# Mixer stage: order of the work at the change of a unit (gate behind the output product, last output product behind the scores, exponentials one step ahead, output weights split two and two)

## The chip, the core and the metric

One core of one Trainium2 chip runs the whole program. The metric is the device time of one execution in microseconds (us). PE is TensorE (PEld its weight loads), ACT ScalarE, DVE VectorE, POOL GpSimd, SP SyncE, which issues the DMAs.

## What is computed

A block of two layers on x of 2 x 512 tokens by 512 channels: attention, a linear map, then the mixer (a state-space layer) and experts, with layer norms between. The change is in the mixer alone. Per token (after the projections to gate, x, B, C and dt), with P = 128 tokens a chunk in this kernel (the chunk length is free, the result doesn't depend on it):

```
x, B, C = silu(conv4(project(input)))           # 128 heads of 64 channels in 8 groups; B, C of 128 channels per group
cum     = cumsum(-exp(A_log) * dt) within a chunk
scores  = (C B^T) * exp(cum_i - cum_j), i >= j
y       = scores @ (dt * x) + exp(cum) * C @ state + D * x
state   = exp(cum_last) * state + B^T @ (dt * exp(cum_last - cum) * x)
y       = y * silu(gate);  y = y / rms over the 1024 channels of the group
out    += y @ out_w[group]
```

Float32 products are made of float32r parts: split_product makes high*high, high*low and low*high, three matmuls per 128 channels of depth, so each weight or activation exists as a high and a low part.

## The kernel before, in words

The mixer (function mixer) has 8 groups x 2 halves = 16 **units** of 8 heads (512 channels). A unit has 8 steps, c = 0 to 7, one per chunk of 128 tokens (chunks 0 to 3 are the first sequence, 4 to 7 the second). A group is 16 steps, k = 0 to 15; k = 0 and k = 8 are the first steps of units. Group 0 and group 7 are written out, groups 1 to 6 are a hardware loop (eng.Fori in groups, L1182). Every engine has its own program, in order, and they meet in semaphores alone; the order of the work is written out by hand.

Products of one step on PE, in this order: at c = 0 and 4 **flip_x** of the chunk itself (four transposes of the convolved channels into p_flip, L1242); in the first half the score product C B^T and a transpose of B (p_mix, L1280, L1281, called cb); the **gate** product (12 matmuls of 128x512 into p_gate); **flip_y** of the step before (L1251); the product with the carried state (p_inter, L1295, not at c = 0 and 4); one or two **channel products** (12 matmuls each into one of two banks of p_mix), which prepare x channels of the next unit or sequence, or B and C of the next group (class Plan says which; two at k = 0, 12, 13 and 14, one at the others); the **output product** of the step before (project_out, 12 matmuls into p_out); the state product (p_state, L1311, not at c = 3 and 7); flip_x of the next chunk (not at c = 3 and 7); and **intra**, the scores by x (16 matmuls, p_intra, L1321). Intra ends a step in the tables here. Three PSUM buffers matter: p_flip is single, so flip_x waits until the flip before it is read out (flip_out), and p_gate and p_out are single too. All eight banks are in use.

ACT in a step: the decay exponentials (L1379, eight of 128x128, behind a table load), at c = 0 and 4 empty_x (p_flip to x_tokens, L1350), the Silu of the gate (L1386, behind a table load), empty_y (p_flip to the high part of yT, L1358), the square of y (L1360), at c = 7 gate_high_part (L1335), the first tap of each convolution (L744), its Silu (activate, L752), keep_half (p_out to half_out, first half only), empty_x of the next chunk, and at c = 0 out_high_part (L1342), the high parts of the unit's output weights, which waits for the output product of the step before. The group's exponentials (L1371) stand ahead of k = 0.

DVE in a step: the arguments of the next step's decays (L1442), copies of cb (L1496, L1497), y_low_part (low part of yT, L1452, which frees p_flip), the carried part (L1512, L1516), mean_square, the other taps (L764, three per convolution), out_sum (L1470, L1473, second half only), the state (L1537 to L1544), then **y_sum** (L1550, waits for intra), **y_done** (L1554, by the gate), and at c = 0 out_low_part, four instructions (L1423). At k = 15 the next group's tables (decay_logs, L1430 to L1433) and arguments follow y_low_part. At the head of each loop pass stand two copies (L1480, L1481).

POOL in a step: x_to_state (L1595), x_dt (L1599), x_skip (L1602), the decays by cb (L1607, after the exponentials), inverse_rms (L1582), at c = 7 gate_low_part (four of L1574), the low parts of the next unit's gate weights; it signals gate_split, for which the gate product of c = 0 waits. At c = 0 SP loads the output weights after gate_split too.

Names in rows: wq_t is the decay buffer, cum_all the arguments' input, x_channels and bc_channels the convolved channels.

## Time and profile before

| what | us |
|---|---|
| median of 3 runs (range) | 2282.54 (2276.7 to 2284.81) |
| the profiled execution | 2285.04 |
| its span, first to last instruction | 2283.3 |
| PE busy in it | 2109.0 (92%) |
| DVE, ACT, POOL busy | 1667.0, 1443.2, 1130.3 |
| mean granted clock | 0.963 |
| the mixer: end of the first intra to end of the last | 417.5 to 2191.6 |

A row of the windows view has: the stretch in us from the span's start, its length, then the busy time (and number of instructions) of PE, PEld, DVE, ACT and POOL, the granted clock, the share of the DMA engines and GB/s; a sum row adds the lengths and the busy times of several stretches. A row of the timeline has the start, the time from first start to last end of the instructions merged in it, the engine, line, operation, tiles, their number (x), and in brackets the engine's idle time before it with what ended it.

### The profile page before, as it was taken

The numbers are of one execution on the slowest core, as the hardware profiler recorded it, in microseconds if no ns is written. First come the engines' busy times: TensorE is split into PE (matmuls) and PEld (weight loads), VectorE is DVE, ScalarE is ACT, GpSimd is POOL, SyncE is SP. The second block draws the span as 40 slices with busy tenths as digits, with TensorE's granted clock in tenths as the row PEclk, the third lists the DMA queues.
The fourth block names the chain that finished last, engine by engine and source line by source line (L and its number), as shares of the span: only waits on it lengthen the run. The fifth ranks groups of instructions, "written<-read, shape, count | busy, mean of one in ns | idle before, by whom it ended". The sixth has DMA issues, their size and how long they took to land. (4 is left out here: it accounts for less than half of the span.)

```text
span 2283.3 us, 35195 instructions
## 1 busy us (share of the span) xinstructions
PE 2109.0 (92%) x10968; PEld 1645.1 (72%) x10968; DVE 1667.0 (73%) x2864; ACT 1443.2 (63%) x2823; POOL 1130.3 (50%) x976
## 2 busy tenths in 40 slices
PE   8999886899999999999999999999999999999868
PEld 4666575687777777777777777777777777777645
DVE  4777584677876787678768877877787778777766
ACT  1566524676667666766676677666766776677631
POOL 3545140455545564555465546564645465545531
PEclk9899997899999999999999999999999999999979
DMA  4000001312122212221222122212121222121110
GB/s 157 1 0 0 23 29 41 97 59 81 47 87 79 68 42 87 84 70 40 87 79 70 57 78 70 70 62 74 70 70 62 74 70 75 56 74 57 46 36 37
DMA packets 72231, 140.67 MB, mean 62 GB/s; under 512 B 34450, under 2 KB 35474, under 8 KB 67827
## 3 DMA queue, kind: packets, MB, share of 16 engines
q1 hardware_dynamic: 72050, 138.44, 18.4%
q8 instruction: 92, 1.51, 0.3%
q14 instruction: 89, 0.72, 0.1%
HBM read 134.74 MB, written 3.67 MB: 61 GB/s over the span
## 5 line engine op out<-in xcount | busy, mean ns | idle before, releaser
L92 PE MATMUL p_out<-w_out,yT 128*128 128x512 f32 x1536 | 391.5, 406 | 44.9 <-DVE yT L1452 38.7
L92 PEld LDWEIGHTS p_out<-w_out,yT 128*128 128x128 f32 x1536 | 298.1, 196 | 121.0 <-DVE yT L1452 43.4
L92 PE MATMUL p_mix<-x_high,w_x 128*128 128x512 f32 x1024 | 381.8, 434 | 1.4 <-DVE x_low L1028 1.4
L1607 POOL TENSOR_TENSOR wq_t<-wq_t,cb 128x1024 f32<-128x1024 f32 x128 | 325.2, 2541 | 108.5 <-DVE cb L1497 96.0
L764 DVE SCALAR_TENSOR_TENSOR conv<-p_mix,unit_small,conv 128x511 f32<-128x511 f32 (+2 forms) x384 | 287.3, 748 | 96.7 <-ACT conv L744 87.6
L92 PE MATMUL p_gate<-w_gate,x_high 128*128 128x512 f32 x1024 | 342.1, 416 | 13.7 <-POOL w_gate L1574 13.7
L1379 ACT ACTIVATE wq_t<-wq_t,minus_cum 128x128 f32<-128x128 f32 x1024 | 313.9, 389 | 1.4
L752 ACT ACTIVATE x_channels<-conv 128x512 f32<-128x512 f32 x128 | 80.6, 630 | 266.4 <-DVE conv L764 265.7
L1452 DVE TENSOR_TENSOR yT<-p_flip,yT 128x512 fp32r<-128x512 f32 x128 | 88.4, 691 | 216.0 <-ACT yT L1358 216.0
L1321 PEld LDWEIGHTS p_intra<-x_dt,wq_t 128*128 128x128 f32 x2048 | 241.1, 192 | 2.4
L1321 PE MATMUL p_intra<-x_dt,wq_t 128*128 128x64 f32 x2048 | 242.6, 272 | 0.0
L92 PEld LDWEIGHTS p_mix<-x_high,w_x 128*128 128x128 f32 x1024 | 194.0, 190 | 62.2 <-issue 22.2
L92 PEld LDWEIGHTS p_gate<-w_gate,x_high 128*128 128x128 f32 x1024 | 190.5, 196 | 52.1 <-POOL w_gate L1574 15.8
L1595 POOL TENSOR_TENSOR x_to_state<-x_tokens,group_dt_end 128x512 f32<-128x512 f32 x96 | 102.7, 1070 | 251.7 <-ACT x_tokens L1350 237.0
L1442 DVE TENSOR_TENSOR wq_t<-cum_all,group_logs 128x1024 f32<-128x1024 f32 x128 | 218.1, 1704 | 2.6 <-DMA cum_all<-cum_rows 1.3
L783 POOL TENSOR_TENSOR w_x<-w_raw_tiles,w_x 128x512 fp32r<-128x512 f32 x64 | 87.4, 1366 | 251.2 <-DVE w_x L772 251.2
L92 PE MATMUL p_gate<-w_gate,x_low 128*128 128x512 f32 x512 | 207.8, 406 | 0.0
L92 PE MATMUL p_mix<-x_low,w_x 128*128 128x512 f32 x512 | 201.2, 393 | 0.0
L1599 POOL TENSOR_TENSOR x_dt<-x_tokens,group_dt 128x512 f32<-128x512 f32 x128 | 143.8, 1124 | 99.9 <-PE p_intra L1321 99.6
L1602 POOL TENSOR_TENSOR x_skip<-x_tokens,group_skip 128x512 f32<-128x512 f32 x128 | 183.2, 1431 | 0.5 <-DVE y L1550 0.5
L744 ACT ACTIVATE conv<-p_mix,unit_small 128x512 f32<-128x512 f32 x128 | 99.7, 779 | 114.9 <-PE p_mix L92 112.9
L1386 ACT ACT_TABLE_LOAD x128 | 164.2, 1283 | 4.9 <-DVE y L1554 2.7
(228 smaller groups left out, 4179.4 us busy)
## 6 DMA issues: line engine op xcount, KB each, us to landing
cum_all<-cum_rows SPq DMA_DIRECT2D x128, 512.0 KB, 3.7
w_staged<-in_w_gate SPq DMA_DIRECT2D x16, 1024.0 KB, 5.8
w_raw_tiles<-in_w_x SPq DMA_DIRECT2D x64, 256.0 KB, 3.7
w_staged<-in_w_out SPq DMA_DIRECT2D x16, 1024.0 KB, 4.8
w_raw_tiles<-in_w_bc SPq DMA_DIRECT2D x16, 256.0 KB, 2.9
x<-in_x SPq DMA_DIRECT2D x1, 2048.0 KB, 17.4
out<-z SPq DMA_DIRECT2D x8, 256.0 KB, 2.0
wqkv<-in_wqkv SPq DMA_DIRECT2D x4, 384.0 KB, 6.3
```

The lines of the kernel that those rows point to most:

```text
L92: last = pe.matmul(dst, left[a](k), right[b](k), start=k == 0 and n_ == 0, stop=stop and k == tiles - 1 and n_ == 2)
L744: act.activation(self.conv[:, par], self.p_mix[:, bank], ACT.Identity, bias=w[:, TAPS:TAPS + 1], scale=w[:, TAPS - 1:TAPS]).then_inc(self. ...
L764: m = dve.scalar_tensor_tensor(self.conv[:, par, back:], self.p_mix[:, bank, 0:SEQ - back], w[:, TAPS - 1 - back:TAPS - back], self.conv[: ...
L1321: m = pe.matmul(p_intra[:, h * HEAD_P:(h + 1) * HEAD_P], decay[:, k % 2, h], xdt[:, h], start=True, stop=True)
L1379: m = act.activation(decay[:, k % 2, h], decay[:, k % 2, h], ACT.Exp, bias=neg[:, c, head:head + 1])
L1386: act.activation(sg[:], p_gate[:], ACT.Silu).then_inc(sg_done, 1)
L1442: dve.tensor_tensor(decay[:, k % 2], cumB[:], over(logs[:, 0, c, mine], P), ALU.min).then_inc(arg_done, 1)
L1452: dve.tensor_tensor(yT[:, 1].rearrange("p j t -> p (j t)"), p_flip[:], yT[:, 0].rearrange("p j t -> p (j t)").bitcast(F32), ALU.subtract). ...
L1595: pool.tensor_tensor(xs[:], xtok[:], over(dtend[:, c, mine], HEAD_P), ALU.mult).then_inc(xs_done, 1)
L1599: pool.tensor_tensor(xdt[:], xtok[:], over(dtg[:, c, mine], HEAD_P), ALU.mult).then_inc(xdt_done, 1)
L1602: pool.tensor_tensor(xskip[:], xtok[:], over(dg[:, mine], HEAD_P), ALU.mult).then_inc(xskip_done, 1)
L1607: pool.tensor_tensor(decay[:, k % 2], decay[:, k % 2], cb[:, c].unsqueeze(1).to_broadcast([P, UNIT_HEADS, P]), ALU.mult).then_inc(decay_do ...
```

## The change

On PE, at c = 0 flip_y and the first channel product come ahead of flip_x, and the gate product comes last, behind the other channel product and the output product. At c = 7 the output product moves behind intra. On ACT the exponentials of the next step move to the end of c = 7 (those of the next group too), with the Silu of the last convolution of the unit taken into the next c = 0. On DVE the arguments at c = 0 come after y_low_part, the next group's tables after the carried part, out_sum at c = 7 to the end of the step; the output weights' low parts are made two before the state and two at the end. On POOL x_skip at c = 0 comes after the decays. flip_index (which flip frees p_flip for which) follows the new order: flip_x at c = 0 now waits for y_low_part.

```diff
 # tensor
+                        if c == CPS:
+                            first_flip(g, k, first)
                         if half == 0:
...
                         if c == 0:
-                            pe.wait_ge(gate_split, g * 2 + half + 1)
-                        wait(pe, sg_done, s)
-                        split_product(pe, p_gate[:], ...).then_inc(gate_done, 1)
...
+                            if before:
+                                flip_y(*before)
+                            conv_event(*convs[0])
+                            first_flip(g, k, first)
+                            for i, e in convs[1:]:
+                                conv_event(i, e)
+                            if before:
+                                project_out(*before)
+                            project_gate(g, k, cols)
+                        else:
+                            project_gate(g, k, cols)
+                            flip_y(*before)
...
+                            for i, e in convs:
+                                conv_event(i, e)
+                            if c < CHUNKS - 1:
+                                project_out(*before)
...
                         m.then_inc(intra_done, 1)
+                        if c == CHUNKS - 1:
+                            project_out(*before)
 # scalar
+                group_exps(0)
+                decay_exps(0, 0)
...
+                        if c == 0:
+                            if before:
+                                empty_y(*before)
+                                late = [e for e in PLAN.events(*before, False) if e[0][0] != "cb"]
+                                for e, _, index in late:
+                                    front.activate(act, e, index, PLAN.conv_parity(before[1], e))
+                                square_y(*before)
+                            empty_x(g, k)
+                            for i, e in convs:
+                                first_tap(i, *e)
+                            front.activate(act, convs[0][1][0], ...)
+                            wait(act, out_done, s)
+                            out_high_part(g * 2 + half, half)
+                            if half:
+                                keep_half(*before)
+                            for i, (e, _, index) in convs[1:]:
+                                front.activate(act, e, index, PLAN.conv_parity(k, e))
+                            silu_gate(g, k)
+                            empty_x(g, k + 1)
+                            continue
...
+                        if c == CHUNKS - 1:
+                            if half and not last:
+                                group_exps(g + 1)
+                            if not (last and half):
+                                decay_exps(s + 1, (k + 1) % STEPS)
+                            if not half:
+                                keep_half(*before)
+                            continue
 # vector
-                        if k + 1 < STEPS:
+                        early = c > 0 and k + 1 < STEPS
+                        if early:
                             arguments(s + 1, k + 1)
...
+                        if c == 0:
+                            arguments(s + 1, k + 1)
...
+                        if c == 0:
+                            out_low_part(g * 2 + half, half, (0, 1))
                         if feeds(c):
...
+                        if summed and c == CHUNKS - 1:
+                            out_sum(*before)
                         if c == 0:
-                            out_low_part(g * 2 + half, half)
+                            out_low_part(g * 2 + half, half, (2, 3))
 # gpsimd
-                        wait(pool, y_sum, s)
-                        pool.tensor_tensor(xskip[:], ...).then_inc(xskip_done, 1)
+                        if c:
+                            skip_part(s, mine)
                         pool.wait_ge(exp_done, s + 1)
...
+                        if c == 0:
+                            skip_part(s, mine)
```

## Rows read from the trace of the kernel before

**Rows 1.** The page's busy times: PE's share of the span.

```profile
PE 2109.0 (92%) x10968; PEld 1645.1 (72%) x10968; DVE 1667.0 (73%) x2864; ACT 1443.2 (63%) x2823; POOL 1130.3 (50%) x976
```

**Rows 2.** Windows of group 4: steps k = 0, 1, 2, 8, 9, 10.

```profile
1303.11:1324.95 21.84, 18.44 (x84) 14.87 (x84) 12.90 (x23) 12.64 (x24) 11.42 (x9) 0.84 0.22 75
1324.95:1339.30 14.35, 13.23 (x69) 10.29 (x69) 12.04 (x17) 11.14 (x22) 5.63 (x5) 1.00 0.44 98
1339.30:1352.24 12.94, 12.94 (x69) 10.37 (x69) 9.79 (x13) 9.25 (x19) 5.27 (x4) 1.00 0.31 112
1414.74:1428.69 13.95, 12.71 (x68) 10.21 (x68) 6.73 (x10) 10.99 (x22) 8.13 (x7) 1.00 0.32 115
1428.69:1446.45 17.76, 14.52 (x65) 11.15 (x65) 16.49 (x19) 11.14 (x21) 8.30 (x7) 0.90 0.33 104
1446.45:1459.10 12.65, 12.65 (x66) 10.08 (x65) 10.55 (x15) 8.72 (x18) 6.33 (x5) 1.00 0.19 62
```

**Rows 3.** Windows of k = 0 and 1: groups 1 and 7 alone.

```profile
626.51:661.40 34.89, 30.30 (x150) 24.28 (x151) 25.75 (x40) 23.78 (x45) 16.89 (x13) 0.95 0.30 84
1978.83:2015.09 36.26, 31.51 (x151) 25.12 (x151) 26.01 (x40) 23.80 (x45) 17.06 (x13) 0.91 0.27 95
```

**Rows 4.** The same for groups 2 to 6, their sum.

```profile
sum 179.92, PE 157.18 PEld 125.39 DVE 124.61 ACT 119.24 POOL 85.08; mean PE 31.44 PEld 25.08 DVE 24.92 ACT 23.85 POOL 17.02
```

**Rows 5.** Windows of k = 8, 9, 10 of all eight groups, their sum.

```profile
sum 356.42, PE 321.19 PEld 252.72 DVE 268.76 ACT 246.66 POOL 179.26; mean PE 40.15 PEld 31.59 DVE 33.59 ACT 30.83 POOL 22.41
```

**Rows 6.** Timeline, PE's waits at both unit changes of group 4 (in brackets).

```profile
1305.70 0.65 PE L1242 MATMUL p_flip<-ident,x_channels 128*128 128x128 f32 x4 [2.58 <-issue]
...
1307.71 1.22 PE L92 MATMUL p_gate<-w_gate,x_high 128*128 128x512 f32 x2 [0.82 <-POOL w_gate L1574]
...
1438.82 4.60 PE L92 MATMUL p_out<-w_out,yT 128*128 128x512 f32 x12 [3.25 <-DVE yT L1452]
```

**Rows 7.** Timeline at the loop's turn: POOL and DVE.

```profile
1301.75 5.91 POOL L1574 TENSOR_TENSOR w_gate<-w_staged,w_gate 128x512 fp32r<-128x512 f32 x4
...
1305.57 0.97 DVE L1554 TENSOR_TENSOR y<-y,silu_gate 128x512 f32<-128x512 f32 x1
...
1309.39 0.23 DVE L1480 COPY group_dt<-tables_in 128x128 f32<-128x128 f32 x1 [2.85 <-issue]
```

**Rows 8.** Timeline from k = 7 into k = 8: POOL, DVE, ACT.

```profile
1407.32 2.44 POOL L1607 TENSOR_TENSOR wq_t<-wq_t,cb 128x1024 f32<-128x1024 f32 x1 [1.56 <-DVE cb L1497]
...
1411.70 2.32 DVE L764 SCALAR_TENSOR_TENSOR conv<-p_mix,unit_small,conv 128x511 f32<-128x511 f32 x3 [1.34 <-ACT conv L744]
...
1414.78 0.69 DVE L1550 TENSOR_TENSOR y<-p_intra,x_skip 128x512 f32<-128x512 f32 x1 [0.76 <-PE p_intra L1321]
...
1416.48 2.45 ACT L1379 ACTIVATE wq_t<-wq_t,minus_cum 128x128 f32<-128x128 f32 x8
...
1419.43 1.28 ACT L1386 ACT_TABLE_LOAD   x1
...
1420.73 0.60 ACT L1386 ACTIVATE silu_gate<-p_gate 128x512 f32<-128x512 f32 x1
```

**Rows 9.** Timeline: out_low_part at k = 0 and at k = 8, then arguments, y_low_part.

```profile
1326.55 3.52 DVE L1423 SCALAR_TENSOR_TENSOR w_out<-w_staged,unit_small,w_out 128x512 fp32r<-128x512 f32 x4
...
1430.58 6.45 DVE L1423 SCALAR_TENSOR_TENSOR w_out<-w_staged,unit_small,w_out 128x512 fp32r<-128x512 f32 x4
...
1436.95 1.21 DVE L1442 TENSOR_TENSOR wq_t<-cum_all,group_logs 128x1024 f32<-128x1024 f32 x1
...
1438.09 0.68 DVE L1452 TENSOR_TENSOR yT<-p_flip,yT 128x512 fp32r<-128x512 f32 x1
```

**Rows 10.** Timeline, PE at the mixer's first gate product, first and last output product.

```profile
403.64 1.22 PE L92 MATMUL p_gate<-w_gate,x_high 128*128 128x512 f32 x2 [4.95 <-POOL w_gate L1574]
...
428.25 0.93 PE L92 MATMUL p_out<-w_out,yT 128*128 128x512 f32 x3 [3.47 <-DVE yT L1452]
...
2195.27 5.48 PE L92 MATMUL p_out<-w_out,yT 128*128 128x512 f32 x12 [1.42 <-DVE yT L1452]
```

More of the change, by code:

```diff
@@ L1261, in project_out, with first_flip, project_gate @@
                                   [lambda j, i=i: wo[:, i, j] for i in range(2)], UT).then_inc(out_done, 1)
+                def first_flip(g, k, first):
+                    pe.wait_ge(conv_done, len(PLAN.first) if first and k == 0 else
+                               PLAN.ready(g, k - 1, ("x", UT - 1, k % CHUNKS // CPS)))
+                    flip_x(g, k)
+                def project_gate(g, k, cols):
+                    if k % CHUNKS == 0:
+                        pe.wait_ge(gate_split, g * 2 + k // CHUNKS + 1)
+                    wait(pe, sg_done, step(g, k))
+                    split_product(pe, p_gate[:], [lambda kk, x=x: x[:, kk, cols] for x in (x_high, x_low)],
+                                  [lambda kk, i=i: wg[:, i, kk] for i in range(2)], KT).then_inc(gate_done, 1)
                 def group(g, first, last):
@@ L1365, in keep_half, with group_exps, decay_exps, silu_gate @@
                     act.activation(half_out[:, k % CHUNKS], p_out[:], ACT.Copy).then_inc(out_free, 1)
-                def group(g, first, last):
+                def group_exps(g):
                     act.wait_ge(logs_done, g * 4 + 4)
-                    wait(act, y_sum, step(g, 0))
+                    wait(act, carried_done, n_carries(g, 0))
                     act.activation(exps[:].rearrange("p a c h -> p (a c h)"), logs[:].rearrange("p a c h -> p (a c h)"),
                                    ACT.Exp).then_inc(exps_done, 1)
+                def decay_exps(s, k):
+                    half, c = divmod(k, CHUNKS)
+                    act.wait_ge(arg_done, s + 1)
+                    for h in range(UNIT_HEADS):
+                        head = half * UNIT_HEADS + h
+                        m = act.activation(decay[:, k % 2, h], decay[:, k % 2, h], ACT.Exp, bias=neg[:, c, head:head + 1])
+                    m.then_inc(exp_done, 1)
+                def silu_gate(g, k):
+                    s = step(g, k)
+                    act.wait_ge(gate_done, s + 1)
+                    wait(act, y_done, s)
+                    act.activation(sg[:], p_gate[:], ACT.Silu).then_inc(sg_done, 1)
+                group_exps(0)
+                decay_exps(0, 0)
+                def group(g, first, last):
                     for k in range(STEPS):
@@ L1375, in group, with first_tap @@
                         s = step(g, k)
[L1376 to L1391 removed]
+                        before = None if first and k == 0 else (g if k else g - 1, (k - 1) % STEPS)
                         target = 1 - half if c >= CPS else half
                         convs = [(i, e) for i, e in enumerate(PLAN.events(g, k, last)) if e[0][0] != "cb"]
[L1394 removed]
+                        def first_tap(i, e, fill, index):
                             if e[0] == "x" and c == CPS:
@@ new lines, in group @@
+                        decay_exps(s, k)
+                        if c == CPS:
+                            empty_x(g, k)
+                        silu_gate(g, k)
+                        empty_y(*before)
+                        square_y(*before)
+                        if c == CHUNKS - 1 and not (last and half):
+                            gate_high_part(g * 2 + half + 1)
+                        for i, e in convs:
+                            first_tap(i, *e)
+                        if c == CHUNKS - 1:
[6 more added lines that the diff above has]
+                            continue
@@ L1401, in group @@
+                        for i, (e, _, index) in convs:
                             front.activate(act, e, index, PLAN.conv_parity(k, e))
-                        if not (first and k == 0) and before[1] < CHUNKS:
+                        if before[1] < CHUNKS:
                             keep_half(*before)
```

103 lines of the change are left out of this document (39 added, 64 removed).

## Prediction, made before the change was run

> **What bounds the kernel now.** The page's busy times come first: PE works 92% of the span [rows 1], and no other engine comes near. So only two things can be won: time in which PE stands still, and time in which it runs at the lower of its clock levels (1.2 instead of 2.4 GHz). Next I read the windows of single steps of one group for where those are. Step k = 2 takes 12.94 us with PE busy for all of it at a clock of 1.00, and k = 10 takes 12.65 in the same way [rows 2]; these are the prices of work alone. One 12-matmul product at the lower level takes 5.48 [rows 10], so 2.74 at the full one, and k = 2 differs from k = 10 by the score product, 0.29. The steps at a change of unit are dearer than their work. k = 0 has 12.4 (below) + 0.29 + 2.74 for its second channel product = 15.4 of work and takes 21.84; its clock of 0.84 means 7.0 us at the lower level, 3.5 lost. k = 1 takes 14.35 for 12.94. k = 8 takes 13.95: its work is at most the busy 12.71, and a little less, since a matmul's modelled end hangs over before a wait; I take 12.4. k = 9 takes 17.76 for 12.65, at a clock of 0.90: 1.8 lost [rows 2].
>
> The timeline then says what PE waited for. At the loop's turn 2.58 is the turn itself (released by nothing but issue), then 0.82 for the low part of the gate weights on POOL; at k = 9 the output product waits 3.25 for y_low_part on DVE and then runs slowly (4.60) [rows 6]. POOL's four w_gate instructions last from 1301.75 to 1307.66 [rows 7], so this wait would end there however short the turn was. On DVE out_low_part (6.45 for four), arguments and y_low_part stand in a row up to 1438.77 [rows 9], just where PE's product starts. Each wait of 2 us or more is followed by the lower clock, while k = 1 with about 1 us of standing still keeps 1.00 [rows 2].
>
> **What the change does, k = 8 first (eight of them).** I walk through group 4, whose k = 7 ends at 1414.74. Intra of k = 7 now comes before the output product: it starts at 1410.1, and the decays are ready at 1409.76 (1407.32 + 2.44, [rows 8]). The output product fills the 2.74 behind it, so PE arrives at 1414.7 as before; this move costs nothing as long as the decays are in time, by 0.3. The taps end at 1414.02 (1411.70 + 2.32), y_sum and y_done take 0.69 and up to 0.97 [rows 7, 8], so y is ready at 1415.6, not 1416.3 as now: flip_y, now first, waits 0.85. The first channel product (2.74) runs to 1418.8. ACT meanwhile (a pass over 128x512 takes it the 0.60 of the Silu, [rows 8]): exponentials of k = 8 behind a table load from 1411.7 to 1415.4 (1.28 + 2.45, [rows 8]), keep_half 0.6, empty_y to 1416.9, then the Silu held over from k = 7, a table load and 0.6: ready at 1418.8, level with PE. y_low_part ends at 1417.5. The flip, the output product (no wait) and the gate product take 0.4 + 2.74 + 2.74, to 1424.7. Beside them go empty_x, the two products and the decays on POOL (1.0 + 1.0 + 2.44; k = 2 has 5.27 for four POOL instructions, the decays among them, [rows 2]) to 1424.7, and intra begins at 1426.0 at the earliest: 1.3 of room. Out_high_part (2.6, after the product at 1422) and the Silu of the gate end near 1427.6, the gate product of k = 9 starts at 1427.9. On DVE two of the four low parts end before intra does. Two are left after y_done (1429.6): 1.8 or 3.2 by the two rows, 0.88 or 1.6 each [rows 9]; I take 3.2, as POOL is at work then, as it is at 1430.58 now. Arguments (1.2 to 2.1) and y_low_part (0.7) end at 1435.5 and PE comes at 1434.7: a wait of 0.8 instead of 3.25. DVE stays late into k = 10 for another 0.35. No wait reaches 2 us, so no lower clock. Steps 8 to 10 are then 12.4 + 12.65 + 12.65 of work and 2.0 of waits, 39.7. The eight now take 356.42 [rows 5]: 356.4 - 8 x 39.7 = **38.8 won**.
>
> **k = 0 in groups 2 to 6, at the loop's turn.** PE arrives at 1303.1 as before and pays the turn, 2.58: that stays, and with it the lower clock. The gate weights no longer matter; POOL ends them at 1305.7 or 1307.7 and the gate product comes near 1318. What is late next is DVE. It ends y_done at 1305.5 and has out_sum behind it (two of 0.75), the last of them issued at 1306.3. Now its first instruction in the new pass starts 3.8 after the issue of the last one of the old (1309.39 against 1305.57, [rows 7]); so 1310.1, then two copies, two of cb, the group's product and y_low_part: 1312.0. The new flip_x waits for that, the old one didn't. PE meanwhile does the score product, flip_y and a channel product, 3.5 of work, which at the lower clock takes it to about the same time. So 8.9 pass to the flip, and 28.4 - 3.5 = 24.9 of work follow (28.4 is 15.4 + 12.94), with 0.4 for a last bit of lower clock: 34.2. Inverse_rms now stands behind the decays and x_skip on POOL, and out_sum waits for it near 1319.5; p_out is needed again only at 1333. k = 1 has no wait left, since half of out_low_part went ahead. Five of these take 179.92 [rows 4]: **8.9 won**, little, since the turn moved from behind one wait to ahead of another.
>
> **Groups 1 and 7** are entered without a turn on DVE; by the same steps y_low_part ends 6.5 after PE's arrival, and 6.5 + 24.9 = 31.4 stand against 34.89 and 36.26 [rows 3]: **8.4 won**. **The first step** now stands still 4.95 for the gate weights [rows 10]; two channel products at the lower clock (5.2 each) fit there, and its intra ends 2.5 earlier. The 3.47 before the first output product and some 1.7 of lower clock behind it become a wait of 1.1: 4.0 more, **6.5**. **The end:** the last product runs at 5.48 after a wait [rows 10]. With the one before it moved behind intra, y is ready when PE is: about 1.4 of waiting and 2.6 of clock, **4.0**.
>
> **At nothing:** the moved exponentials of a new group (k = 15, ACT idle before its last Silu), the tables on DVE (the same 1 us, two places later), out_sum at c = 7, x_skip behind the decays (hidden under the gate product; y_sum wants it 2 us later), and SP, whose loads follow the same signals: the output weights, asked for when POOL ends, land some 8 us ahead of need. If these covers went, each costs up to its own 1 to 2.5 us at 15 changes.
>
> **A rule against it.** The Silu held over puts a table load between flip_y and flip_x. By the row the next activation starts 0.02 after the load of 1.28 ends [rows 8]. The Trainium skill, "ScalarE: Activation LUTs", What ACT_TABLE_LOAD costs, gives about 1.38 us of DRAIN on top of each switch; with that, 1.3 at 15 changes, the time would be some 20 us higher. The trace shows no such stretch.
>
> **The sum.** 38.8 + 8.9 + 8.4 + 6.5 + 4.0 = 66.6, off the profiled execution's own 2285.0: **2218**. The median of the runs shown is 2.5 below that execution, well inside their spread; I stay with the sum. About 0.3% is what a measurement of this kernel tells from no change.
>
> **Rivals.**
> (a) *The covers are thinner than I think* (0.3 at the decays of k = 7, none at the held-over Silu, 1.3 at the decays of k = 8). DVE and ACT rows show instructions that take half as long again in company [rows 9]. With 2 us more at each of 15 changes: 2218 + 30 = 2248. Chance 0.22.
> (b) *The first flip becomes the bound, and the time rises.* It now waits for three things in a row, y_done, y_low_part and the held-over Silu. If this wait is 2.5 at every change and brings the lower clock with it for the 7 us seen at k = 0 (3.4 lost), that is 5.9 x 15 = 88 against 66.6: 2307. It decides from 4.4 per change. Against it: PE has a channel product of 2.74 to do meanwhile, and standing still for 1 us never cost clock here. Chance 0.05.
> (c) *More is won:* DVE's low parts run at 0.88, and its turn is hidden. The waits left are 16 at k = 8 to 10, 5 x 3.2 at the turns and 6 in groups 1 and 7, 38 in all; with half of them gone 2199. Chance 0.14.
> (d) *No change:* every wait comes back one product later, because DVE, not the order, sets the change of unit. DVE is busy 16.49 of 17.76 at k = 9 [rows 2]. But it falls to 10.55 of 12.65 right after, and its low parts are spread now. 2283; chance 0.04.
> My forecast has 0.55. The range from 2196 to 2254 takes in (a) and (c), the second low parts at 0.88 or 1.6 each (11 us over eight) and the turn with 3.4 or 7 us of lower clock. Faster 0.91, the same 0.04, slower 0.05.
>
> **What would show it.** Right: k = 8 to 10 near 39.7 with a clock of 1.00; no wait on w_gate; in the loop 34 for k = 0 and 1, with issue and then DVE yT ahead of the first flip; PE still busy about 2105 less the clock won (some 30). Wrong: waits on the decays at k = 7, on x_channels or on POOL before intra of k = 0 or 8, and a clock below 0.95 at k = 8 or 9.

## The result, and the profile after

| | before | after |
|---|---|---|
| median of the runs, us | 2282.54 (5 runs, 2276.7 to 2284.81) | 2263.56 (5 runs, 2261.41 to 2267.16) |
| span of the profiled execution | 2283.3 | 2261.1 |
| mean granted clock | 0.963 | 0.972 |

The ratio is 0.9926, interval 0.9914 to 0.9938: the change makes the kernel 0.74% faster, which is clear of the noise but small, where 2.9% was forecast. The spans of the two profiled executions differ by 22.2 us, a third of the 66.6 of the sum.

The page's busy times, against [rows 1]:

```profile
PE 2096.3 (93%) x10968; PEld 1632.1 (72%) x10968; DVE 1724.3 (76%) x2864; ACT 1444.1 (64%) x2823; POOL 1140.0 (50%) x976
```

DVE executes the same 2864 instructions as before and is busy 57 us longer (1667.0 before). That is the first sign: the change gave it no work, so its instructions became slower.

The waits view of PE says in a few rows what the change took away and what it put there. Columns: who waited, for whom, us in total, times, the longest. First the kernel before, then after:

```profile
PE p_out L92 <- DVE yT L1452: 38.7, 18, 3.5
PE p_flip L1251 <- ACT x_tokens L1350: 18.6, 24, 1.3
PE p_gate L92 <- POOL w_gate L1574: 13.7, 8, 5.0
PE p_flip L1242 <- issue: 13.5, 5, 2.9
...
PE p_flip L1251 <- DVE y L1554: 2.4, 2, 1.6
```

```profile
PE p_flip L1252 <- DVE y L1623: 41.9, 29, 2.9
PE p_out L92 <- DVE yT L1515: 18.0, 11, 2.4
...
PE p_flip L1243 <- DVE yT L1515: 10.7, 5, 2.3
```

The wait on w_gate is gone and the one on y_low_part before the output product is halved, but the flips of y, which used to wait 2.4 us in all for y_done, now wait 41.9 for it (their waits on ACT's x_tokens fell from 18.6 to 9.0), and the first flip_x waits 10.7 for y_low_part.

Since the output product of c = 7 moved across the end of a step, whole stretches have to be compared: k = 7 to 10 (a "half" below), and k = 15, 0 and 1, which contain the loop's turn, the way from the end of one pass to the start of the next (a "turn" below). Sums of the windows view, before: the turns of groups 2 to 6, then k = 7 to 10 of all eight groups, then groups 1 and 7:

```profile
sum 238.35, PE 214.96 PEld 170.91 DVE 168.18 ACT 161.19 POOL 124.98; mean PE 14.33 PEld 11.39 DVE 11.21 ACT 10.75 POOL 8.33
...
sum 449.56, PE 414.32 PEld 328.45 DVE 334.86 ACT 320.39 POOL 258.60; mean PE 12.95 PEld 10.26 DVE 10.46 ACT 10.01 POOL 8.08
...
sum 94.41, PE 84.93 PEld 67.60 DVE 69.24 ACT 64.37 POOL 49.97; mean PE 14.15 PEld 11.27 DVE 11.54 ACT 10.73 POOL 8.33
```

The same sums after:

```profile
sum 241.34, PE 216.32 PEld 171.04 DVE 178.20 ACT 161.42 POOL 125.22; mean PE 14.42 PEld 11.40 DVE 11.88 ACT 10.76 POOL 8.35
...
sum 440.74, PE 402.90 PEld 317.10 DVE 379.32 ACT 320.46 POOL 263.17; mean PE 12.59 PEld 9.91 DVE 11.85 ACT 10.01 POOL 8.22
...
sum 86.54, PE 81.76 PEld 65.71 DVE 70.46 ACT 64.59 POOL 50.65; mean PE 13.63 PEld 10.95 DVE 11.74 ACT 10.77 POOL 8.44
```

| stretch | forecast, won | measured, won |
|---|---|---|
| k = 7 to 10, eight | 38.8 | 8.8 |
| turns, groups 2 to 6 | 8.9 | -3.0 |
| groups 1 and 7 | 8.4 | 7.9 |
| first step | 6.5 | 6.6 |
| end and the rest of the span | 4.0 | 1.9 |

Two terms failed, by 30 and by 12. The single steps of group 4 show where (windows of k = 0, 1, 7, 8, 9 and 10, against [rows 2]):

```profile
1283.29:1310.13 26.84, 21.85 (x96) 16.98 (x95) 18.05 (x28) 14.89 (x27) 12.28 (x10) 0.87 0.23 81
1310.13:1323.07 12.94, 12.94 (x70) 10.37 (x69) 11.65 (x15) 8.70 (x19) 5.54 (x5) 1.00 0.44 97
...
1386.87:1395.78 8.91, 8.91 (x51) 7.36 (x50) 6.33 (x10) 8.85 (x20) 7.20 (x5) 1.00 0.36 118
1395.78:1412.19 16.41, 15.33 (x79) 12.19 (x79) 12.50 (x14) 13.06 (x26) 10.92 (x9) 1.00 0.26 97
1412.19:1428.31 16.12, 13.14 (x65) 9.93 (x65) 15.84 (x18) 9.38 (x18) 9.17 (x7) 1.00 0.32 111
1428.31:1442.17 13.86, 12.86 (x65) 10.00 (x65) 13.51 (x17) 8.76 (x18) 5.98 (x5) 1.00 0.16 61
```

The clock is 1.00 through this half, as forecast (of the eight, only k = 9 of the first group is at 0.90), and k = 1 has lost its wait. k = 9 takes 16.12 with 3.0 of standing still, k = 10 takes 13.86 with 1.0. The timeline of DVE, POOL and PE across k = 8 and 9 names the cause (against [rows 9] and the last of [rows 6]):

```profile
1407.26 3.10 DVE L776 CAST w_bc<-w_raw_tiles 128x512 fp32r<-128x512 f32 x2
...
1410.05 3.15 POOL L788 TENSOR_TENSOR w_bc<-w_raw_tiles,w_bc 128x512 fp32r<-128x512 f32 x2
1410.29 3.46 DVE L1487 SCALAR_TENSOR_TENSOR w_out<-w_staged,unit_small,w_out 128x512 fp32r<-128x512 f32 x2
...
1415.05 1.15 DVE L1623 TENSOR_TENSOR y<-y,silu_gate 128x512 f32<-128x512 f32 x1
...
1416.12 4.35 DVE L1487 SCALAR_TENSOR_TENSOR w_out<-w_staged,unit_small,w_out 128x512 fp32r<-128x512 f32 x2
1416.33 0.66 PE L1252 MATMUL p_flip<-ident,y 128*128 128x128 f32 x4 [1.32 <-DVE y L1623]
...
1421.53 0.68 DVE L1515 TENSOR_TENSOR yT<-p_flip,yT 128x512 fp32r<-128x512 f32 x1
...
1422.26 3.02 PE L92 MATMUL p_out<-w_out,yT 128*128 128x512 f32 x12 [1.66 <-DVE yT L1515]
```

The two copies w_bc (high parts of the B and C weights) take 3.10 beside POOL's decays and x_skip; before they took 0.76, at a place where POOL mostly stood still. The two early low parts take 3.46 beside POOL's w_bc, the late two 4.35, where I had 3.2. So y_done comes late for the flip of k = 9, and y_low_part for the output product. Group 7 has no w_bc work, and there k = 9 takes 14.50 in the same trace. DVE's groups of the lines view (busy us, mean ns of one), before and after:

```profile
L1442 DVE TENSOR_TENSOR wq_t<-cum_all,group_logs 128x1024 f32<-128x1024 f32 x128 | 218.1, 1704 | 2.6 <-DMA cum_all<-cum_rows 1.3 <-DVE group_logs L1433 1.2
L1550 DVE TENSOR_TENSOR y<-p_intra,x_skip 128x512 f32<-128x512 f32 x128 | 88.0, 687 | 58.4 <-PE p_intra L1321 58.4
L1423 DVE SCALAR_TENSOR_TENSOR w_out<-w_staged,unit_small,w_out 128x512 fp32r<-128x512 f32 x64 | 77.5, 1269 | 0.0
...
L776 DVE CAST w_bc<-w_raw_tiles 128x512 fp32r<-128x512 f32 x16 | 6.1, 420 | 0.0
```

```profile
L1505 DVE TENSOR_TENSOR wq_t<-cum_all,group_logs 128x1024 f32<-128x1024 f32 x128 | 232.7, 1818 | 1.3 <-DVE group_logs L1496 1.2
L1487 DVE SCALAR_TENSOR_TENSOR w_out<-w_staged,unit_small,w_out 128x512 fp32r<-128x512 f32 x64 | 91.5, 1469 | 1.3 <-ACT w_out L1360 1.3
L1619 DVE TENSOR_TENSOR y<-p_intra,x_skip 128x512 f32<-128x512 f32 x128 | 87.6, 684 | 45.0 <-PE p_intra L1337 45.0
...
L776 DVE CAST w_bc<-w_raw_tiles 128x512 fp32r<-128x512 f32 x16 | 22.6, 1444 | 0.0
```

y_sum, which takes one input from PSUM, keeps its 0.69; the copy from SBUF to SBUF and the forms with two inputs in SBUF got longer. The Trainium skill, "SBUF — State Buffer", SBUF: two separate sides, says that DVE and GpSimd share a port pair as an exclusive lock, which a DVE operation takes in a two-port mode or, against a GpSimd operation that reads SBUF, with two SBUF inputs. By that, y_sum is untouched and the others can be held up; the trace agrees. That it is this lock, and not something else that the two engines share, no run here shows.

At the loop's turn of group 4 (timeline of SP, POOL, DVE, PE, against the first rows of [rows 6] and [rows 7]):

```profile
1282.75 5.97 POOL L1645 TENSOR_TENSOR w_gate<-w_staged,w_gate 128x512 fp32r<-128x512 f32 x4
1282.91 2.20 DVE L1505 TENSOR_TENSOR wq_t<-cum_all,group_logs 128x1024 f32<-128x1024 f32 x1 [0.20 <-DVE group_logs L1496]
...
1288.04 1.23 DVE L1623 TENSOR_TENSOR y<-y,silu_gate 128x512 f32<-128x512 f32 x1
1288.88 0.33 SPq L696 DMA_DIRECT2D w_staged<-in_w_out  x1
...
1289.41 0.65 PE L1252 MATMUL p_flip<-ident,y 128*128 128x128 f32 x4 [2.66 <-DVE y L1623]
...
1289.97 0.75 DVE L1536 SCALAR_TENSOR_TENSOR acc<-attn,inv_rms,acc 128x512 f32<-128x512 f32 x1
...
1295.10 0.23 DVE L1543 COPY group_dt<-tables_in 128x128 f32<-128x128 f32 x1 [4.38 <-issue]
...
1295.91 0.68 DVE L1515 TENSOR_TENSOR yT<-p_flip,yT 128x512 fp32r<-128x512 f32 x1
...
1296.65 0.66 PE L1243 MATMUL p_flip<-ident,x_channels 128*128 128x128 f32 x4 [2.24 <-DVE yT L1515]
```

PE's own turn is no longer seen: its queued output product runs meanwhile. But PE stands still 2.66 for y_done and 2.24 for y_low_part, with a stretch at the lower clock behind each. DVE's turn, from the start of its last instruction to the first of the new pass, takes 5.1, where I had 3.8. Its last instruction starts 1.1 behind SP's load of the output weights.

### The profile page after: what moved, and what is told of

Same layout as the page of the kernel before. It is cut to its first block and busy times, and to the rows that moved or that the text cites. A ratio compares the mean times of both kernels' runs of the same rounds, so it can differ in the third digit from the quotient of the medians.

```text
span 2261.1 us, 35194 instructions
## 1 busy us (share of the span) xinstructions
PE 2096.3 (93%) x10968; PEld 1632.1 (72%) x10968; DVE 1724.3 (76%) x2864; ACT 1444.1 (64%) x2823; POOL 1140.0 (50%) x976
## 5 line engine op out<-in xcount | busy, mean ns | idle before, releaser
L92 PE MATMUL p_out<-w_out,yT 128*128 128x512 f32 x1536 | 380.0, 397 | 21.4 <-DVE yT L1515 18.0
L92 PE MATMUL p_mix<-x_high,w_x 128*128 128x512 f32 x1024 | 388.3, 441 | 1.4 <-DVE x_low L1028 1.4
L92 PEld LDWEIGHTS p_out<-w_out,yT 128*128 128x128 f32 x1536 | 288.3, 190 | 89.7 <-DVE yT L1515 22.6
L92 PE MATMUL p_gate<-w_gate,x_high 128*128 128x512 f32 x1024 | 327.5, 401 | 0.2 <-ACT silu_gate L1408 0.2
L92 PEld LDWEIGHTS p_mix<-x_high,w_x 128*128 128x128 f32 x1024 | 198.5, 194 | 63.5 <-issue 22.2
L1337 PE MATMUL p_intra<-x_dt,wq_t 128*128 128x64 f32 x2048 | 242.7, 272 | 1.0 <-POOL wq_t L1682 1.0
L1505 DVE TENSOR_TENSOR wq_t<-cum_all,group_logs 128x1024 f32<-128x1024 f32 x128 | 232.7, 1818 | 1.3 <-DVE group_logs L1496 1.2
L92 PEld LDWEIGHTS p_gate<-w_gate,x_high 128*128 128x128 f32 x1024 | 184.2, 189 | 35.0 <-ACT silu_gate L1408 0.4
L92 PE MATMUL p_gate<-w_gate,x_low 128*128 128x512 f32 x512 | 201.4, 393 | 0.0
```

What stands on the lines that cost most here:

```text
L92: last = pe.matmul(dst, left[a](k), right[b](k), start=k == 0 and n_ == 0, stop=stop and k == tiles - 1 and n_ == 2)
L1337: m = pe.matmul(p_intra[:, h * HEAD_P:(h + 1) * HEAD_P], decay[:, k % 2, h], xdt[:, h], start=True, stop=True)
L1505: dve.tensor_tensor(decay[:, k % 2], cumB[:], over(logs[:, 0, c, mine], P), ALU.min).then_inc(arg_done, 1)
```

## The experiments

Medians of runs beside the kernel before on the same chip; that kernel's own median was 2279.3 to 2283.4 beside the experiments, so between sets of runs the ratios compare better than the medians. The last two columns are the sums of the windows of k = 15, 0, 1 in groups 2 to 6 and of k = 7 to 10 in all groups, in the profiled execution.

| kernel | median | ratio to before [interval] | turns | halves |
|---|---|---|---|---|
| before | 2282.54 | | 238.4 | 449.6 |
| the change | 2263.56 | 0.9926 [0.9914, 0.9938] | 241.3 | 440.7 |
| lows_together | 2271.06 | 0.9949 [0.9933, 0.9965] | 242.9 | 445.8 |
| product_back | 2269.36 | 0.9943 [0.9928, 0.9958] | 237.4 | 448.1 |
| gate_first | 2281.19 | 0.9997 [0.9982, 1.0012] | 228.3 | 457.9 |
| hoist | 2247.04 | 0.9850 [0.9823, 0.9877] | 226.9 | 440.3 |
| sum_late | 2241.90 | 0.9824 [0.9808, 0.9840] | 223.2 | 440.9 |
| bc_early | 2254.05 | 0.9866 [0.9841, 0.9891] | 242.7 | 434.3 |
| hoist_bc | 2240.02 | 0.9819 [0.9797, 0.9840] | 227.4 | 429.6 |
| hoist_bc_low | 2238.01 | 0.9812 [0.9796, 0.9829] | 226.5 | 429.0 |
| pool_light | 2239.58 | 0.9814 [0.9791, 0.9837] | 239.6 | 417.1 |
| sum_bc | 2231.19 | 0.9775 [0.9755, 0.9796] | 219.4 | 431.2 |
| sum_bc_args | 2245.34 | 0.9839 [0.9819, 0.9859] | 219.5 | 445.5 |
| sum_bc_low_args | 2231.69 | 0.9774 [0.9752, 0.9796] | 217.9 | 433.4 |
| load_late | 2246.68 | 0.9858 [0.9836, 0.9880] | 226.5 | 440.8 |
| light_sum | 2222.19 | 0.9746 [0.9724, 0.9768] | 222.9 | 417.0 |
| sum_bc_load | 2228.54 | 0.9779 [0.9756, 0.9802] | 218.1 | 429.4 |

**Single parts undone.** Each is the changed kernel with one edit.

```diff
 # lows_together
-                        if c == 0:
-                            out_low_part(g * 2 + half, half, (0, 1))
...
-                            out_low_part(g * 2 + half, half, (2, 3))
+                            out_low_part(g * 2 + half, half, range(UT))
 # product_back
-                            if c < CHUNKS - 1:
-                                project_out(*before)
+                            project_out(*before)
...
-                        if c == CHUNKS - 1:
-                            project_out(*before)
 # gate_first
                         if c == 0:
+                            project_gate(g, k, cols)
...
-                            project_gate(g, k, cols)
```

> The changed kernel (2263.6 us) with all four low parts of the output weights at the end of k = 0 and 8 again, as before the change. Theory A (DVE's chain through the change of unit sets PE's waits, and its instructions run long beside POOL's): the two parts only change their place in one chain; the wait ahead of flip_y at k = 9 (1.3) goes, the one ahead of the output product (1.7) grows by as much or more: 2260 to 2272. Theory B (the split is what won at k = 1 and 9): 1.8 to 3.4 us at 15 changes come back: 2285 or more, with waits over 3 us and the lower clock at k = 9.

2271.06, 7.5 above the change and inside theory A's range: with all four low parts behind y_done the output product of k = 9 in group 4 waits 3.41 (3.25 in [rows 6]) and runs at the lower clock. So it goes in seven of the eight groups. In group 1 the same product waits 3.39 and the clock stays at 1.00: a wait of this length doesn't always bring the lower clock.

> The changed kernel with the output product at c = 7 ahead of the scores again, as before the change. Theory A: intra of c = 7 ends 2.7 us later, y_sum waits for it instead of for the taps, y_done comes 0.9 us later and PE's wait ahead of flip_y grows from 1.1 to about 2: 15 x 0.9, 2277. Rival (DVE is late by the taps anyway): no change, 2264.

2269.36, 5.8 above, between the two numbers. The halves lose 7.4 (the flip at k = 8 waits 1.66 instead of 1.08, and the output product lies ahead of intra again, where it delays the whole chain to y); the turns gain 4.0. In three of the eight halves that wait of 1.66 is followed by the lower clock (0.89 over k = 8), in the others the clock stays at 1.00.

> The changed kernel with the gate product at c = 0 ahead of flip_y again (the rest of the new order kept). Theory A: at the loop's turn PE waits 1.9 us for POOL's w_gate and does the gate product while DVE makes y and turns; the waits of 2.7 and 2.2 us there shrink to about 2 in all, 3 us won at five turns; at k = 8 flip_x comes 2.4 us later, POOL's decays too, 0.9 us lost at eight changes: 2256. Rival (the gate product behind the output product is what won the 19 us): the waits of before on w_gate come back, 2275 to 2282.

2281.19: all that the change won is lost, so my theory's 2256 was wrong and the rival's 2275 to 2282 held. The gate product then waits 1.85 on w_gate at the turn, which still makes the turns 13.1 shorter, but the halves are 17.1 longer, k = 1 takes 14.25 again and k = 0 and 1 of the first group about 3 more each. The gate product behind the output product is what pays, in the halves and in the first group.

**The turn.** hoist puts y_low_part, the two head copies, cb and the group's product ahead of the branch and out_sum(14) behind it; sum_late only the last:

```diff
 # sum_late (and hoist)
-                        if summed and c == CHUNKS - 1:
+                        if summed and c == CHUNKS - 1 and last:
                             out_sum(*before)
...
+                        if k == 0 and not first:
+                            out_sum(g - 1, STEPS - 2)
 # hoist besides: at the end of the pass, and left out at the head of the next
+                        if k == STEPS - 1 and not last:
+                            head(g + 1)
+                            empty_cb(g + 1, 0)
+                            end_factor(g + 1)
+                            y_low_part(g, k)
```

> The changed kernel with DVE's y_low_part of k = 15, the head of the group and the copies of cb of k = 0 ahead of the loop's turn, and out_sum of k = 14 behind it. Theory A (y_low_part behind DVE's turn of some 5 us holds the first flip): the wait of 2.2 us ahead of flip_x and the second stretch of lower clock (1.7) go at five turns, 15 to 20 us: 2244 to 2249. Rival (PE would wait for the next thing from DVE, the taps or the arguments, just as long): 2260 to 2265.

2247.04, inside what was expected. The wait of flip_x for y_low_part has no row in PE's waits any more.

> The changed kernel (2263.6) with out_sum of k = 14 behind the loop's turn on DVE (the rest of DVE's order as changed). It tells how much of the 16.5 us that the version with y_low_part ahead of the turn won is out_sum's 1.5 us ahead of the turn. Theory A: DVE turns 1.5 us earlier, the wait ahead of the first flip falls from 2.2 to about 0.7, five times 1.5, and the second stretch of lower clock may go: 2248 to 2256. Rival (the turn's length, not its start, decides; DVE's first instruction comes at the same time): 2263.

2241.90, 21.7 below the change, more than expected, and no less than hoist (the intervals overlap). The timeline of DVE in group 4:

```profile
1282.30 1.22 DVE L1625 TENSOR_TENSOR y<-y,silu_gate 128x512 f32<-128x512 f32 x1
1285.73 0.23 DVE L1543 COPY group_dt<-tables_in 128x128 f32<-128x128 f32 x1 [2.21 <-issue]
```

The turn is not only earlier by the out_sum, it is 3.4 long instead of 5.1. Moving one cheap pair of instructions from before the branch to behind it won 21.7, the whole change 19.0. Why the turn is shorter was still open: in all kernels it was long where SP had issued the 1 MB load of the output weights shortly before the branch. The next run moves that load alone:

```diff
 # load_late
                             sp.wait_ge(gate_split, g * 2 + half + 1)
+                            if k == 0 and not first:
+                                sp.wait_ge(group_done, g * 3 + 2)
                             front.to_stage(sp, d["w_out"][:, half], g, 0)
```

> Edit: the changed kernel, but SP's 1 MB load of the output weights at k = 0 waits also for the first two copies of DVE in the new pass (not in the first group). Nothing else is different. In all kernels so far the DVE turn is long (4.6 to 5.2 us from the last instruction's issue to the first of the new pass) where this load was issued about 1.2 us before the branch, 3.3 to 4.2 where it was 2.4 before, and short (2.8 to 3.6) where it was issued 0.7 to 2.2 behind it. Then the turn falls to 3.0 to 3.6, y_low_part ends 1.7 earlier, the 2.2 before the first flip_x shrinks to about 0.5 and perhaps one of the two stretches at the lower clock goes: 2 to 4 us at five turns, 2244 to 2254. The load then lands near 1300 of group 4, 4 us ahead of its first use. Rival U: the length goes by the instruction ahead of the branch (out_sum 4.6 to 5.2, y 2.8 to 3.6, y_low_part 3.4 to 4.2): then the turn stays at 5 and the time at 2261 to 2266.

2246.68, by theory T. The timeline of DVE and SP in group 4, with out_sum ahead of the branch as in the change:

```profile
1282.25 0.75 DVE L1538 SCALAR_TENSOR_TENSOR acc<-attn,inv_rms,acc 128x512 f32<-128x512 f32 x1
...
1285.54 0.23 DVE L1545 COPY group_dt<-tables_in 128x128 f32<-128x128 f32 x1 [2.54 <-issue]
...
1286.02 0.33 SPq L696 DMA_DIRECT2D w_staged<-in_w_out  x1
```

3.3 from start to start, with the same instruction in front. So the load in flight stretches the turn; the instruction ahead of it does not. The other kernels bear it out: where the load was issued 1.1 before the start of the last instruction (the change and five of the experiments), the five turns each last 4.5 to 5.4; where it was issued behind it (the kernel before and seven experiments), 3.1 to 3.8. The three kernels with hoist's edit, which have y_low_part ahead of the branch, are left out here. The DMA view of the changed kernel, from 1282 to 1300 us, shows packets of instructions beside those of the load (q1), all as shares of the same 16 DMA engines:

```profile
q1 hardware_dynamic: 367, 1.90, 29.7%
q8 instruction: 2, 0.03, 0.7%
q14 instruction: 4, 0.03, 0.6%
```

That these few packets stand behind the load's is my reading; the view doesn't say which engine they are for.

**DVE beside POOL.** bc_early moves the w_bc copies to where DVE waits for the first tap of k = 8; pool_light leaves DVE alone and thins POOL (x_skip of k = 8 to 10 is made for one head of eight and the low parts of the B and C weights for 8 columns, so it doesn't compute the block; it is a measuring kernel, and so is light_sum):

```diff
 # bc_early: from ahead of the first out_low_part to
+                        if k == CHUNKS and not last:
+                            for j in range(2):
+                                front.bc_high_part(dve, g * 5 + 6, j)
 # pool_light
+                    n_ = 1 if mine.start and light else UNIT_HEADS
+                    pool.tensor_tensor(xskip[:, :n_], xtok[:, :n_], over(dg[:, mine], HEAD_P)[:, :n_], ...)
...
-                                front.bc_low_part(pool, g + 1, j)
+                                pool.tensor_tensor(front.wbc[:, 1, j, 0:1, 0:8], ...)
```

> The changed kernel with DVE's two copies w_bc of k = 8 in DVE's idle time ahead of the taps, where POOL stands still. Theory C (DVE's instructions run long because they now lie beside POOL's x_to_state, x_dt and decays): the pair falls from 3.1 to about 0.8 us, y_done of k = 8 comes 1.3 earlier, the wait ahead of flip_y at k = 9 goes: seven times 1 to 1.3, 2255. Rival (DVE's low parts are the bound at k = 9 anyway, the time only moves into the next wait): 2261 to 2264, with the wait ahead of the output product of k = 9 grown by as much.

2254.05. The copies are back at 421 ns and k = 9 falls from 16.12 to 13.2, but k = 10 rises to between 14.7 and 16.4: its flip now waits 1.88 for y_done. Of the 2.9 us a half 0.8 is left in the mean (halves 6.4 shorter in all).

> The changed kernel with some of POOL's work at the change of halves left out and nothing of DVE's touched: x_skip at k = 8 to 10 is made for one head of eight, and the low parts of the B and C weights for 8 columns, so y and B, C are not those of the reference. Theory C (DVE's instructions are long because of POOL's beside them): with the same DVE instructions, its low parts of the output weights at k = 8 and 9, y by gate and the arguments fall towards 0.9, 0.7 and 1.2 us, and the waits of 1.3, 1.7 and 1.0 us at k = 9 and 10 shrink to 1.5 in all: 2243 to 2252. Rival (DVE has simply too many instructions there, whatever POOL does): 2260 or more, and the waits stay. Another (POOL, not DVE, is what PE waits for through the decays): the waits at k = 9 and 10 go, but DVE's durations stay.

2239.58, 24.0 below the change, with every instruction of DVE in its place. Its lines view:

```profile
L1505 DVE TENSOR_TENSOR wq_t<-cum_all,group_logs 128x1024 f32<-128x1024 f32 x128 | 251.0, 1961 | 1.3 <-DVE group_logs L1496 1.2
...
L1487 DVE SCALAR_TENSOR_TENSOR w_out<-w_staged,unit_small,w_out 128x512 fp32r<-128x512 f32 x64 | 57.8, 943 | 1.3 <-ACT w_out L1360 1.3
...
L776 DVE CAST w_bc<-w_raw_tiles 128x512 fp32r<-128x512 f32 x16 | 17.3, 1119 | 0.0
```

The low parts fall from 1469 to 943 ns. k = 9 takes 13.73 and its output product waits 0.80. That this is the very number of the forecast is luck: the w_bc copies, which the forecast left out, are still long here, and the late low parts are shorter than its 3.2. (The mean of the arguments rises to 1961.)

> Edit: pool_light (it leaves out 7/8 of x_skip at k = 8 to 10 and most of the low parts of the B and C weights on POOL, so the output is not the reference's) and sum_late (out_sum(14) behind the turn) in one. The forecast of 2218 failed by 45.6. If the two things named were the whole of it (DVE beside POOL in steps 8 to 10, worth 24.0 alone; out_sum ahead of DVE's turn, worth 21.7 alone) and they add, this kernel takes 2263.6 - 24.0 - 21.7 = 2218 (2214 to 2222). Rival: a next wait takes over part of it, or the two share gains: 2225 to 2235.

The edits of pool_light and sum_late in one: 2222.19, just above what was expected. The stretches add up: turns 222.9 as in sum_late, halves 417.0 as in pool_light. The spans of the profiled executions say the same: 2238.6 and 2243.9 alone are 22.5 and 17.2 below the 2261.1 of the change, together 39.7, and this one has 2220.5, which is 40.6 below. The medians add less neatly: 24.0 and 21.7 alone, 41.4 together. The missing 4 us are about what the intervals leave open, so a small overlap is neither shown nor excluded.

**Towards a better kernel.**

> The version with y_low_part ahead of the turn (2247) and the w_bc copies in DVE's idle time together. Theories A and C act at different places (turn, k = 8), so the gains add: 2238 to 2242. Rival: 2247.

> The same, and POOL's two w_bc low parts (3.2 us) moved from k = 8 to behind the decays of k = 9, where POOL stands still for 4 us. Theory C: DVE's low parts of the output weights and y_done at k = 8 then run beside less, 0.9 instead of 1.7 each for the first two; another 1 to 2 us at seven changes: 2228 to 2236. Rival (DVE's length does not come from POOL): the same as the version before it, within 2 us, with the low parts at 1.7 to 2.2 each.

2240.02 and 2238.01: hoist and bc_early in one, both edits as above. The second has POOL's low parts of w_bc one step later besides:

```diff
-                        if k == CHUNKS and not last:
+                        if k == CHUNKS + 1 and not last:
```

The halves win 10 to 11 on hoist. hoist_bc came as expected; hoist_bc_low missed its 2228 to 2236, and what it adds over the first can't be told from nothing (the intervals overlap). In group 4, k = 9 rose from 13.26 to 14.50 and k = 10 fell from 16.40 to 13.88: the wait changed its step.

> The changed kernel with out_sum of k = 14 behind the turn (2241.9 alone) and the w_bc copies in DVE's idle time (2254 alone, 9.5 less than the changed kernel). The two act at different places, so 2231 to 2236. Rival (the turn gets longer again with what comes before it, as with y_low_part ahead of it): 2240.

> The same, and DVE's arguments at k = 1 and 9 behind y_low_part instead of ahead of it (the output product waits for y_low_part, the arguments are wanted a step later). DVE's chain at k = 9 is low parts, arguments (up to 3.4 us beside POOL), y_low_part: 1 us at most is left of the wait ahead of the output product in each group's k = 9, but y of k = 9 stays late at k = 10. It would give 0 to 1 us at eight changes where the copies w_bc are early already: 2225 to 2235. Rival: no change against the version before it.

> The same again, and POOL's two w_bc low parts behind the decays of k = 9. There the arguments ahead of y_low_part ran 3.5 us beside POOL's decays and PE waited 1.6 for y_low_part; with the order changed that wait goes: 2218 to 2228. Rival (the next wait, flip_y at k = 10, takes it over in full): 2232 or more.

sum_bc is sum_late with bc_early, both edits as above: 2231.19. The two others put the arguments of k = 1 and 9 behind y_low_part:

```diff
 # sum_bc_args, sum_bc_low_args
-                        early = c > 0 and k + 1 < STEPS
+                        early = c > 1 and k + 1 < STEPS
...
-                        if c == 0:
+                        if c < 2:
                             arguments(s + 1, k + 1)
```

Both missed what was expected. In sum_bc_args (2245.34) k = 9 has its 12.7 of pure work in the loop's groups, but k = 10 takes 16 to 19, with 3.31 of waiting before its flip in group 4 and the lower clock behind it. PE's first row in the waits view of sum_bc_args:

```profile
PE p_flip L1252 <- DVE y L1625: 51.2, 23, 3.3
```

With POOL's low parts later, as in hoist_bc_low (sum_bc_low_args, 2231.69), it is 2.20, and nothing is left over against sum_bc. The next wait took the gain over.

> Edit: sum_bc (out_sum(14) behind the turn, the copies of the B and C weights' high parts early in k = 8) and the late load of load_late. The load was issued 0.7 us behind DVE's branch here and the turn is already 2.8 to 3.2. Theory T: nothing or a little, up to 0.4 at five turns, 2229 to 2232 (sum_bc had 2231.2). Rival: the load, 3 us later, comes after its need (out_high_part on ACT waits, the gate product behind it): slower by 1 to 2 at five turns, 2236 to 2241.

The edit of load_late in sum_bc: 2228.54 against a kernel before that was 3.5 lower in these runs; by the ratio (0.9779 and 0.9775) it is the same as sum_bc. The turn was short there already. The best kernels that compute the whole block, sum_bc, sum_bc_low_args and sum_bc_load, can't be told apart; they are 2.2 to 2.3% below the kernel before and 1.5% below the change (0.9775 / 0.9926).

## Why the prediction was right in direction and wrong in size

**The direction** held: what bounds the kernel is PE's waits. **The price of standing still** held only in the main. In the changed kernel the waits of 1.0 to 1.7 us in the halves were followed by no lower clock, and a wait of 1.79 was (before the output product of k = 9 in the first group, whose k = 9 takes 17.67 for 16.12). But one length of wait goes both ways: in sum_bc k = 10 waits 1.9 in the six groups of the loop and takes 16.4 in three of them and 14.7 in the others, and product_back and lows_together show the same at 1.66 and 3.4. "Each wait of 2 us or more is followed by the lower clock" was also a wrong reading of the kernel before. Its output product at k = 12 of group 7 waits 2.40 and runs at full speed; after the change the same wait is followed by the lower clock:

```profile
2151.15 3.02 PE L92 MATMUL p_out<-w_out,yT 128*128 128x512 f32 x12 [2.40 <-DVE yT L1452]
```

```profile
2130.89 4.37 PE L92 MATMUL p_out<-w_out,yT 128*128 128x512 f32 x12 [2.40 <-DVE yT L1515]
```

What decides it these runs don't show.

**k = 8 to 10, 38.8 forecast, 8.8 measured.** k = 7 and 8 came as worked out: 8.91 + 16.41 is 25.3, for 24.9. No wait for the decays shows at k = 7. The held-over Silu was ready at 1402.91 and flip_x of k = 8 began at 1403.04, right behind the channel product; the Silu itself started at 1402.28, 0.02 after its table load (1400.98 and 1.28 long). By the rule weighed in the forecast (the Trainium skill, "ScalarE: Activation LUTs", What ACT_TABLE_LOAD costs) 1.38 of DRAIN would stand between the two; the trace has none here either. The step that failed was "On DVE two of the four low parts end before intra does" with the 3.2 for the others. The w_bc copies, which stand right ahead of the low parts, had no term in my list at all. They were 0.76 before only because POOL was idle there; the new order of PE and the later x_skip moved POOL's decays and x_skip onto them (3.10) and POOL's work onto all four low parts (3.46 + 4.35; the forecast had 3.2 for the late two and nothing that PE would see for the early two). Nor did these end before intra: they ran until 1413.75, intra until 1412.19. The 0.8 before the output product of k = 9 became 1.66, with 1.32 before its flip, for which I had nothing, and 1.0 in k = 10 for 0.35. pool_light puts DVE's durations near those that I used, and 23.6 of the missing 30 come back (440.7 to 417.1; the forecast is 449.6 - 38.8 = 410.8). The rest, some 6, is spread over small things that no run takes apart, such as 1.08 at k = 8 for 0.85, and k = 9 and 10 of pool_light each 0.1 to 0.3 over the forecast.

**The turns, 8.9 forecast, 3.0 lost.** The step "its first instruction in the new pass starts 3.8 after the issue of the last one" took a length from the trace and carried it to a place where something else ran beside it. With out_sum in front, DVE's last instruction started 1.1 after SP's 1 MB load and not 2.3 before it as in the old order, and the turn took 5.1. load_late gives it back: 14.8 of the turns' sum (241.3 to 226.5, below the 229.5 forecast). I also had flip_y at the turn without a wait. It waits 2.66, and ahead of y_done DVE still has the next group's tables and arguments (2.20 beside w_gate on POOL), while PE's own turn, which used to cover them, was now hidden; no run moves them, so their share of the 2.66 is argued and not shown. That PE would pay its 2.58 was wrong, but nothing was won by it: the wait for y_done has the same size.

**Groups 1 and 7 and the first step** came out within 0.5. **The end** won 1.9 of 4.0: k = 12 of group 7 lost 1.3 to the lower clock behind the wait of 2.40 shown above, which the change didn't make. bc_early and load_late have the same wait and keep their clock, so this 1.3 can't be charged to the change. Without it some 3.2 would have been won.

**The rivals.** Rival (a) had the right cause, instructions that take longer in company, at the wrong places: not at the covers of the decays and the Silu (both held) but on DVE between y_done and y_low_part. Its 2248 was closer than 2218 by another way than its own, and 2263.6 lies above the range, since I took company as a risk of 2 us and not as what happens by default where the order pushes POOL and DVE together. (b) came true in part at the loop's turn alone: in group 4 the two flips wait 2.66 and 2.24 there, each with the lower clock behind it, while the first flip at k = 8 waits 1.08. (c) and (d) did not happen, though (d) had the right engine: gate_first shows that the order on PE matters, pool_light that DVE takes most of it back.

## What to carry to other kernels

An order that closes an engine's gaps pushes the other engines' work together: before moving work, list every DVE instruction of the stretch with two SBUF inputs or a copy from SBUF to SBUF, the ones not edited too, and price them at their length beside POOL. Keep the last instructions ahead of a loop's branch few, and keep large loads away from the branch. Where a wait is removed, look at the following two steps: the copies moved early won 2.9 at k = 9 and gave back most of it at k = 10; the arguments moved late (sum_bc_args) won 0.5 at k = 9 and lost more at k = 10.

## What was not expected of the hardware

The same CAST of 128x512 on DVE took 0.42 us with POOL mostly idle and 1.44 in the mean beside it, the arguments of 128x1024 took 1.21 at the shortest and 3.40 at the longest. The DVE turn of the loop took 3.3 us or 5.1 with the same instruction in front, by whether a 1 MB load had been issued just before it. PE's turn, 2.58 us in the open before, vanished behind 12 queued matmuls. And the same wait of PE, 1.66, 1.9, 2.40 or 3.4 us long, was followed by the lower clock in one place and not in another.
